# Host-side layout of every input, a split round trip of the counts, and a new order on all engines of a fused attention, FFN and expert kernel

## The reference, cut to what matters

```python
x = x + L0_xattn(ctx, layernorm(x), mask, b)        # 8 heads of 16, K and V are the two halves of ctx
x = x + L0_ffn(layernorm(x), k0, k1, k2, s0, s1, s2) # weights are +1/-1 by boolean arrays, relu, 128-512-512-128
x = x + L1_xattn(layernorm(x), ctx, lens, W_in, b_in, g_res, g_init)
x = x + L1_ffn(layernorm(x), W, b, Wg, bg)           # 8 experts, softmax gate, the best two weighed and added

def L1_xattn(embeds, patch_embeds, patch_lens, ...):
    h = einsum('bld,ed->ble', rmsnorm(embeds, g_res), W_in) + b_in
    # depool: counts where patches end (cumsum of patch_lens), running maximum picks the patch of a position
    return depool(rmsnorm(patch_embeds, g_init)) + h
```

## Time and profile before

| | |
|---|---|
| median of 3 runs | 539.66 us (539.65, 539.66, 540.94) |
| the profiled execution's own time | 538.97 us |
| its span, first to last instruction | 537.2 us |
| PE busy | 497.7 us, 93% of the span |
| DVE, POOL, ACT busy | 433.1, 364.5, 356.7 us |
| mean granted TensorE clock | 0.982 |

### The profile page before, as it was taken

The page is one execution under the profiler, slowest core; times in us unless marked ns, Lnnn a source line. Parts: engine busy times, 40 slices in busy tenths (PEclk is TensorE's granted clock), DMA queues, the critical chain, the costliest instruction groups (busy, mean ns, idle before and its releaser), DMA issues.

```text
span 537.2 us, 15110 instructions
## 1 busy us (share of the span) xinstructions
PE 497.7 (93%) x5549; PEld 324.0 (60%) x5549; DVE 433.1 (81%) x1404; ACT 356.7 (66%) x761; POOL 364.5 (68%) x633
## 2 busy tenths in 40 slices
PE   1756999999999999999999999999999999999893
PEld 1645565666656565766666566666666666655551
DVE  4735868899897979888897979799887785867897
ACT  3398698887967867677686866777566665655410
POOL 7644444588858869686868778686845857654865
PEclk9987899999999999999999999999999999999997
DMA  7402101010310101010110101000000000100010
GB/s 170 101 4 55 32 16 56 2 51 6 82 36 18 34 22 51 23 50 21 31 43 21 52 1 51 21 21 27 3 21 1 2 22 1 33 1 21 1 31 29
DMA packets 28503, 16.98 MB, mean 32 GB/s; under 512 B 3687, under 2 KB 28429, under 8 KB 28430
## 3 DMA queue, kind: packets, MB, share of 16 engines
q1 hardware_dynamic: 26670, 15.57, 10.5%
q10 hardware_dynamic: 1760, 0.46, 0.4%
HBM read 11.74 MB, written 4.24 MB: 30 GB/s over the span
## 4 chain that ended last, share of the span: by engine, by line
PE 64%; DVE 5%; issue 1%; ACT 0%; DVEq 0%
PE ps L2186 16%; PE ps L2134 16%; PE ps L2145 4%; PE ps L2079 4%; PE ps L2022 4%; PE ps L2096 4%; PE ps L2127 4%; PE ps L2164 2%; PE ps L2165 2%; PE ps L2104 2%; PE ps L2054 2%; PE ps L2177 2%; DVE weighed L1046 1%; PE ps L2083 1%; PE ps L2047 1%
## 5 line engine op out<-in xcount | busy, mean ns | idle before, releaser
L2186 PE MATMUL ps<-w_moeT,y4T 128*128 128x512 f32 x256 | 123.5, 607 | 1.2 <-DVE gd L1005 1.1
L613 POOL TENSOR_TENSOR sum<-weighed 128x512 f32<-128x512 f32 x60 | 76.1, 1269 | 71.2 <-DVE weighed L1046 71.2
L2134 PE MATMUL ps<-h,w 128*128 128x512 f16 x512 | 118.6, 379 | 0.0
L1638 ACT ACTIVATE h<-ps 128x512 f16<-128x512 f32 x128 | 74.1, 591 | 46.9 <-PE ps L2134 35.9
L1046 DVE TENSOR_TENSOR weighed<-ps,wgt 128x1024 f32<-128x1024 f32 x64 | 77.8, 1218 | 31.7 <-PE ps L2186 30.7
L969 DVE SCALAR_TENSOR_TENSOR h<-ps,h 128x512 f16<-128x512 f32 x128 | 85.6, 682 | 20.2 <-ACT h L1638 20.1
L2134 PEld LDWEIGHTS ps<-h,w 128*128 128x128 f16 x512 | 48.3, 98 | 56.2 <-issue 5.6
L1604 ACT ACTIVATE prT<-ps,maskT 77x1024 f32<-77x1024 f32 x64 | 67.3, 1101 | 14.8 <-PE ps L2083 14.5
L2186 PEld LDWEIGHTS ps<-w_moeT,y4T 128*128 128x128 f32 x256 | 45.1, 189 | 43.0 <-issue 35.0
L565 POOL TENSOR_TENSOR rs<-ve,neg_half 128x4 f32<-128x4 f32 x64 | 64.9, 1013 | 8.7
L560 POOL TENSOR_TENSOR ve<-mv,eps 128x4 f32<-128x4 f32 x64 | 14.2, 222 | 60.6 <-DVE mv L903 60.4
(11 more groups left out here) (171 smaller groups left out, 986.1 us busy)
## 6 DMA issues: line engine op xcount, KB each, us to landing
cx<-in_ctx SPq DMA_DIRECT2D x16, 308.0 KB
xa<-in_x SPq DMA_DIRECT2D x16, 256.0 KB, 3.0
out_x<-xo SPq DMA_DIRECT2D x16, 256.0 KB, 2.3
plugs<-plug_d SPq DMA_DIRECT2D x16, 77.0 KB
nat<-in_L_ffn_W SPq DMA_DIRECT2D x1, 512.0 KB
k_u<-in_L_ffn_k ACTq DMA_DIRECT2D x1, 256.0 KB, 3.9
k_u<-in_L_ffn_k ACTq DMA_DIRECT2D x1, 128.0 KB, 3.4
k_u<-in_L_ffn_k ACTq DMA_DIRECT2D x1, 64.0 KB, 4.6
```

The source lines that it names most:

```text
L613: nc.gpsimd.tensor_tensor(sum4[:], both[:, 0:4 * D], both[:, 4 * D:8 * D], ALU.add).then_inc(c_sum4.sem, 1)
L1638: last = nc.scalar.activation(h[:, 0, (k - 1) % FC, :], src, ACT.Relu)
L2134: last = pe.matmul(pb(g, k), w2[:, i, c * 128:(c + 1) * 128], h1[:, g.p, part, i, :], start=(i == 0 and part == 0), stop=(i == FC - 1 and ...
L2186: last = pe.matmul(pm(g, j)[:, half, :], y4T[:, g.p, j * S:(j + 1) * S], w_moeT[:, half * 512:(half + 1) * 512], start=True, stop=True)
```

## The change

All inputs are laid out anew on the host, in `laid_out()`, and the results are put back in order there. In the device program:

- x and the result are read and written as `[16][128][512]`, so that a partition's row is one piece of 2048 bytes, not four of 512. The context likewise has rows of 4096 bytes (`load_context`). The keys come transposed, twice, with zeros in the places of the other head (`load_keys`, 128 x 616 to `kT`), the values with their ones and zeros (`load_values`, 77 x 1024 to `vx`). So `a_turn_keys`, `a_keys`, `a_values_in` and `make_values` are gone, and two loads per group are new.
- The weights come transposed: rows 0 to 126 of `w_T` (127 partitions x 1160 columns) in one load, the last row repeated on 128 partitions in a second load, the biases in a third. `turn_weights` and `take_weights` are gone; POOL subtracts in `make_sums_zero`. The mask comes transposed as well.
- The scale of the queries moves from the keys to `a_queries`. The FFN's weights are made by DVE instead of ACT (`make_weights`). DVE normalises part a of groups 1, 2 and 3, and half of part c of group 15.
- `order_counts` is split into `counts_out` and `counts_in`, and `plugs_out` stands apart from `plug(g[0])`, each with loads in between.
- The sums of the experts in the last two groups: DVE adds j = 1 and 3 of group 14 and j = 2 and 3 of group 15 by eight multiply-and-add steps from PSUM (`e_accumulate`). Of group 15, j = 1 is weighed by ACT in eight pieces and summed by nine matmuls on PE (`e_sum`), and copied out by ACT (`e_take`). `keep_busy` is gone.
- All five lists are written anew.

```diff
             def load_rows(g):
...
-                sp.dma_start(xa[:, g.f, :].rearrange("s (j d) -> s j d", j=G),
-                             x[g.n * G:(g.n + 1) * G].rearrange("j s d -> s j d")).then_inc(rows_in[g.f].sem, 16)
+                sp.dma_start(xa[:, g.f, :], x[g.n]).then_inc(rows_in[g.f].sem, 16)
 
             def load_keys(g):
+
+                if g.has(2):
+                    sp.wait_ge(a_less[1].sem, a_less[1].of(g, back=2))
+                sp.dma_start(kT[:, g.p], keys[g.n]).then_inc(keys_in[g.p].sem, 16)
+
+            def load_values(g):
+
+                if g.has(2):
+                    sp.wait_ge(a_pv.sem, a_pv.of(g, back=2))
+                sp.dma_start(vx[:, g.p], values[g.n]).then_inc(values_in[g.p].sem, 16)
...
             def load_weights():
-                for dst, src in ((nat[:, 0:E, :], w_moe.rearrange("e o d -> o e d")), (nat[:, E, :], w_in),
-                                 (nat_gate[:], w_gate), (gres[:], bcast(g_res, 128))):
-                    sp.dma_start(dst, src).then_inc(weights_in, 16)
...
+                sp.dma_start(w_T[0:D - 1, :], weights[0, 0:D - 1, :]).then_inc(weights_in, 16)
+                sp.dma_start(last_row[:], weights[1]).then_inc(weights_in, 16)
+                sp.dma_start(w_T[D - 1:D, :], biases.rearrange("(o d) -> o d", o=1)).then_inc(biases_in, 16)
+
+            def load_gains():
+                sp.dma_start(gres[:], gains).then_inc(weights_in, 16)
+                sp.dma_start(gpatch[:], patch_gains).then_inc(gains_in, 16)
                 sp.dma_start(battn[:], bcast(b_attn, 128)).then_inc(gains_in, 16)
...
-            def order_counts():
+            def counts_out():
 
                 sp.wait_ge(s_counts.sem, 1)
                 sp.dma_start(mark_d.rearrange("b (a c) -> a b c", c=E), counts[:]).then_inc(plug_out, 16)
+
+            def counts_in():
                 sp.wait_ge(plug_out, 16)
                 sp.dma_start(marked[:], mark_d).then_inc(marks_in, 16)
...
@@ pool @@
-            def make_weights_to_turn():
-                pool.wait_ge(weights_in, 64)
+            def make_sums_zero():
+
+                pool.wait_ge(weights_in, 48)
                 nc.gpsimd.tensor_scalar(gres[:], gres[:], (1 + RMS_EPS) ** -0.5, None, ALU.mult).then_inc(made_w, 1)
...
@@ vector @@
+            def make_weights():
+                dve.wait_ge(made_s, 6)
+                dve.wait_ge(made_halves, 1)
+                nc.vector.tensor_scalar(w1[:], k0_d[:], s_sgn[:, 7:8], None, ALU.mult)
+                nc.vector.tensor_scalar(w2[:], k1_u[:], s_sgn[:, 5:6], s_sgn[:, 6:7], ALU.mult, ALU.add)
+                nc.vector.tensor_scalar(w3[:], k2_u[:], 2.0, -1.0, ALU.mult, ALU.add).then_inc(made_ffn, 1)
...
+            def a_normalise(g):
+
+                dve.wait_ge(ln_a.rs.sem, ln_a.rs.of(g))
...
+            def e_accumulate(g, j, half):
...
+                for e in range(4 * half, 4 * half + 4):
+                    so_far = xo if e else xd
+                    if e:
+                        dve.wait_ge(v_step.sem, v_steps(g, j) + e)
+                    last = nc.vector.scalar_tensor_tensor(xo[:, g.p, cols], pm(g, j)[:, e // 4, (e % 4) * D:(e % 4 + 1) * D],
+                                                          wgt[:, g.p, j, e:e + 1], so_far[:, g.p, cols], ALU.mult, ALU.add)
+                    last.then_inc(v_step.sem if e < E - 1 else c_weighed.sem, 1)
...
             a_stats(g[0])
...
+            a_highest(g[0], 1)
+            a_split_maxima(g[0])
             take_counts()
             make_halves()
...
             a_highest(g[1], 0)
+            make_weights()
+            a_stats(g[2])
+            make_plug()
+            a_stats(g[3])
             a_highest(g[1], 1)
-            a_stats(g[2])
-            a_stats(g[3])
+            a_normalise(g[2])
             a_split_maxima(g[1])
+            a_normalise(g[3])
             a_weigh(g[0])
             a_residual(g[0])
             b_stats(g[0])
-            make_plug()
...
@@ tensor @@
-            def a_turn_keys(g, *readers):
-                free(*readers)
-                pe.wait_ge(keys_in[g.f].sem, 16 * g.quarter + 16)
-                turn4(pa(g)[:, 3, :], lambda j: cx[:, g.f, j, 0:D], NK).then_inc(a_cT.sem, 1)
-
...
+            def e_sum(g, j, *readers):
+
+                free(*readers)
+                pe.wait_ge(s_weighed.sem, s_weighed.of(g, j + 1))
+                pe.wait_ge(c_x3.sem, c_x3.of(g))
+                dst = pm(g, j)[:, 0, 0:D]
+                for e in range(E):
+                    pe.matmul(dst, ident[:], weighed[:, place(g, j), e * D:(e + 1) * D], start=(e == 0), stop=False)
+                pe.matmul(dst, ident[:], xd[:, g.p, j * D:(j + 1) * D], start=False, stop=True).then_inc(s_sum.sem, 1)
...
```

More of the change, by code:

```diff
@@ L60, in turned_at, with build @@
         return self.turned.of(g, self.k, back)
[L63 to L68, removed]
-    G = 4
-    NG = B // G
+def build(nc, x, ctx, keys, values, mask, mask_turned, lens, b_attn, signs, scales, weights, biases, gains, patch_gains, out):
+    B, NK = mask.shape
+    G = 4
+    NG, S, D = x.shape[0], x.shape[1], x.shape[2] // G
+    DC = ctx.shape[2] // G
+    FC = 4
+    F = FC * D
+    assert signs.shape[1] == (2 + FC) * F + FC * D
+    E = weights.shape[2] // D - 1
     HD = D // HEADS
@@ new lines, in count, with place, place_free @@
+        def count(kind, g, j):
+            return sum(1 for i, k in sums_of if how(i)[k] in kind and (i.n, k) <= (g.n, j))
+        def place(g, j):
+            return buffered.index((g.n, j)) % 2
+        def place_free(g, j):
+            n, k = buffered[buffered.index((g.n, j)) - 2]
+            if how(Group(n))[k] == "scalar":
+                return s_sum.sem, s_sum.of(Group(n), k + 1)
+            return c_sum4.sem, added(Group(n), k)
+        def added(g, j):
+            return count(("gpsimd",), g, j)
@@ L908, in a_stats @@
                 stats(ln_a, g, xa[:, g.f, :])
+            def a_normalise(g):
+                dve.wait_ge(ln_a.rs.sem, ln_a.rs.of(g))
+                if g.has(2):
+                    dve.wait_ge(a_xT.sem, a_xT.of(g, back=2))
+                for j in range(G):
+                    last = nc.vector.tensor_scalar(xn[0][:, g.p, j * D:(j + 1) * D], xa[:, g.f, j * D:(j + 1) * D],
+                                                   mv[0][:, g.p, j, 0:1], rs[0][:, g.p, j:j + 1], ALU.subtract, ALU.mult)
+                last.then_inc(a_xn_v.sem, 1)
             def a_highest(g, q):
@@ new lines, in normalise_rest @@
+            def normalise_rest(ln, g, src):
+                n, p = ln.n, g.p
+                dve.wait_ge(ln.rs.sem, ln.rs.of(g))
+                dve.wait_ge(ln.turned.sem, ln.turned_at(g, back=2))
+                for j in range(2, G):
+                    last = nc.vector.tensor_scalar(xn[n][:, p, j * D:(j + 1) * D], src[:, j * D:(j + 1) * D],
+                                                   mv[n][:, p, j, 0:1], rs[n][:, p, j:j + 1], ALU.subtract, ALU.mult)
+                last.then_inc(ln_rest[n].sem, 1)
@@ L1134, in _ @@
             b_low(g[2], 0)
+            a_stats(g[6])
             c_stats(g[1])
@@ L1274, in _ @@
             b_low(g[7], 1)
+            a_stats(g[11])
             b_low(g[7], 2)
@@ L1782, in _ @@
             b_high(g[4], 1)
+            a_decays(g[4])
             b_high(g[4], 2)
```

1432 lines of the change are left out of this document (774 added, 658 removed).

## The result

The changed kernel takes 550.36 us (median of 4 runs, 548.29 to 552.2), the kernel before 540.3 beside it: ratio 1.0185, 95% interval 1.0143 to 1.0227. It is slower by some 10 us, and outside the range that was given.

| | start of b_layer(g0,5) | from there to c_turns(g15) | from there to the end |
|---|---|---|---|
| before, profiled | 63.99 | 444.89 | 28.3 |
| predicted | 73 | 438.8 | 25.7 |
| after, profiled | 75.96 | 444.84 | 26.9 |

The account below looks back on a forecast made before the run. PE's work bounds the body, chains of waits the start and end. From 538.97 us, start +9.0, body -6.1 and end -2.6 gave 539.3; as the profiled execution was 0.7 below the median, 540.0 us was predicted, range 530 to 549.

Parts of the forecast that it names:

- The start, +9.0: Up to b_layer(g[0], 5): the 127-row weights load on one DMA engine delays group 2's rows; 63.99 becomes 73 us.
- the rival with the long hole: Start: the engine shares time with other traffic, 18.6 GB/s, load 8.1 us longer; 548 us in all; chance 0.20.
- a clock that has risen by then: From the FFN's transposes to b_layer(g[0], 5): 12.1 us instead of 13.9, less key transposes and with PE's clock up again.
- If all loads came in time ... the milestone at 54: -10: Start without late loads: FFN transposes at about 40 us instead of 50.08, b_layer(g[0], 5) at 54, 10 us gained.
- the first rival: Start: no single-engine load, the weights spread over engines like others; start gains 10, 521 us in all; chance 0.12.
- Of the 5.2 us of gaps I credit 2.2: Body, b_layer(g[0], 5) to c_turns(g[15]): new lists close 2.2 us of PE's gaps; ends 0 and 5.2, a loss possible.
- the mark of an error: Sign for the body: the prediction is wrong if PE's gaps there are over 6 us.
- The clock in the body: Body: PE was taken to run at full clock, with no term for a drop.
- 12 x 0.27 = 3.2 us less: Body: twelve key transpositions on PE, groups 4 to 15, fall away at 0.27 us each.
- the 0.65 of `keep_busy`: Body: one `keep_busy` of three products ahead of c_turns(g[15]) falls away, 0.65 us less PE work.
- The end: After c_turns(g[15]): -2.6 us; DVE's work behind `wgt` falls from 9.5 to 6.3 us, one weighing and 16 steps.
- The clock in the end: End: without `keep_busy` the last 16 products start at 1.2 GHz, about 5 us late; 545 us in all; chance 0.05.

Follow-up runs that it names:

- Experiment 1: Changed kernel with the biases put in as row 127 of the weights' table, so one load brings 128 rows: 535.84 us, 536.46 when run again.
- Experiment 2: Changed kernel with the same 127 weight rows brought in two loads of 112 and 15 rows: 535.51 us.
- Experiment 4: Kernel before the change, with its load of the experts' weights cut into 127 rows and 1 row: 550.17 us.
- Experiment 8: 128-row weights load, with group 1's maxima split ahead of group 2's normalising at the start: 534.64 us; with the later picks of groups 3 and 6 too: 531.59 us.
- experiment 10: 128-row load, later picks and reordered start, with DVE's start order changed once more (group 1's second maxima and split ahead of the plug): 530.31 us.
- experiment 7: 128-row weights load, with DVE's picks of groups 3 and 6 moved behind those groups' layer 4: 532.16 us.
- Experiment 5: Kernel before the change, with keys of groups 4 to 15 laid out by the host, their transposes and copies gone: 539.19 us, ratio 0.9999.

## Why the prediction was wrong

- **The start, +9.0.** The single-engine load was right in kind, place and rate: one engine, about 26 GB/s (25 taken), a wait at `a_stats(g[2])`, until 42.92 (41.5). Experiments 1, 2 and 4 show it from three sides. That the time came near the rival with the long hole is chance: its rate of 18.6 GB/s did not occur. The term should have been +12.0. The wait ended 1.4 us later; the way from there to `b_turns(g[0])` took 19.7 us (19.4 taken); and from 62.60 to the milestone it took 13.4 us where 12.1 were put down for "a clock that has risen by then". It had not stayed up: the column reads 0.81 and 0.77 in the two stretches of 4 us from 62 to 70 us, and the four products at 64.76 take 1.86 us, where two take 0.59 in the body.
- **"If all loads came in time ... the milestone at 54: -10"** failed. It is no term of the sum, but it carried the first rival's 521 us. Experiment 1 has all loads in time and its milestone at 62.72, so the start without the hole is worth -1.3, and the hole itself costs 75.96 - 62.72 = 13.2 us, not 19. What was taken off was what goes; DVE's new list was not laid out for that case. In it the making of the FFN's weights (from 27.49 to 29.56 us, ACT's work before), two groups' statistics and the plug stand ahead of group 1's second maxima, which come at 32.64 instead of 27.66. Experiments 8 and 10 take part of this away and get only 1.8 us for it. Where the other 7 us went isn't shown; the waits in experiment 10 are for DVE's normalising and for ACT's exponent.
- **"Of the 5.2 us of gaps I credit 2.2"** is the term of the body that failed: it had the wrong sign. PE is busy for 438.20 of 444.84 us, so the gaps are 6.6 us instead of 3.0, over the 6 that were named as the mark of an error. 4.1 of them are waits for `weighed` (experiment 7 shows the cause for half of these).
- **The clock in the body** was put at nothing, and cost about 1.8 us: PEclk reads 0.65 from 152 to 156 us, behind the longest wait, and PE is busy for 438.20 us instead of the 436.43 of experiment 1. That it did not fall in experiment 1 is no merit of that kernel, since it fell when the same kernel ran again.
- **"12 x 0.27 = 3.2 us less"**, with the 0.65 of `keep_busy`, came nearly whole as work: 436.43 us of PE in experiment 1 against 439.68, 3.2 less instead of 3.85. But what made it a gain was not in the prediction. Experiment 5 takes the same transposes out of the old order and gets 0.0, because they covered the wait for `y3T`, and a covered wait has no row. Only in the new order are the rounds 0.22 us shorter. In the changed kernel these gains pay for the gaps and the clock, and no more.
- **The end:** "6.3" behind `wgt` were 7.5 (from 537.67 to 545.13 us), by steps of 0.38 us instead of 0.32. The step had been taken from an add of 0.28; the new ones take 2.67 us for seven:

```profile
538.85 0.34 DVE L1217 SCALAR_TENSOR_TENSOR xo<-ps,wgt,xd 128x128 f32<-128x128 f32 x1
539.23 2.67 DVE L1217 SCALAR_TENSOR_TENSOR xo<-ps,wgt,xo 128x128 f32<-128x128 f32 x7
...
542.46 2.67 DVE L1217 SCALAR_TENSOR_TENSOR xo<-ps,wgt,xo 128x128 f32<-128x128 f32 x7
```

- **The clock in the end** (0.05) didn't come in the changed kernel, but it did in the profiles of two of its variants, for 1.3 us (28.2 instead of 26.9) where the rival had 5.

By parts the error is +3.0, +6.0 and +1.2 us, all of one sign. The body was the largest: +3.6 for gaps, +1.8 for the clock and +0.6 for work. The prediction had named a loss in the gaps as possible and still counted them as a gain, and the clock behind a long wait had no term in the body.

What stays open: which piece of the new order lets the round become 0.22 us shorter, how far the start could be brought down, and why the clock falls in one execution of a kernel and not in another.

## What to carry to other kernels

Before a load is cut to an unusual number of rows, look at what divides that number: filling one row up (here with the biases) or cutting the load in two gave back some 14.5 us, while moving it made things worse. Work that is taken off a full engine is a gain only if nothing waits beneath it; lay out what the engine would wait for in its place. Before a difference of 1 or 2 us is put down to a change, look whether the clock fell in one of the two profiles; the same kernel can show both. And in a list that is made anew, look for DVE's work on two SBUF operands beside GpSimd's, right ahead of what PE waits for.

## What the runs showed of the hardware that was not expected

- SyncE itself stands behind such a load: the next issue took 14.28 us, in the later place 10.27, and in the kernel before with 127 + 1 rows 25.99 for the two issues. So loads behind it are late already in their issue. That a load of 127 rows gets one engine is what the Trainium skill says (DMA: Bandwidth & Descriptors, "Why a DMA increments its semaphore by 16 and not by 1"), and the runs agree, for rows of 4640 bytes in one piece and for rows of eight pieces of 512.
- One engine alone moved about 29 / (16 x 0.07) = 26 GB/s with rows of 4640 bytes, and about 22 / (16 x 0.08) = 17 with pieces of 512.
- A DVE operation on 32 columns took 1.21 or 1.36 us instead of 0.19 beside a GpSimd operation, and a GpSimd add of 128 columns 0.90 instead of 0.45 beside DVE's `pick`.
- PE's clock fell in the middle of the full body, behind a wait of only 2.5 us, and in one run behind 8 us with 0.6 us of gaps (PE busy 7.41 of 8), each time for some 4 to 8 us and at a price of 1.3 to 1.8 us. Behind one and the same wait of 2.5 us it fell in one profile of a kernel and not in the other.
